# Attention scores in bf16 six-part stacks, and in fp32r three-part stacks with two heads in the row halves of the array

## The reference

```
A:   q, k, v = x @ Wq, x @ Wk, x @ Wv        # 32 query heads, 8 key/value heads, head size 16
     q, k = rope(q), rope(k)
B:   q, k, v = x @ Wq.T + bq, ...            # 32 heads of size 16, no rope
both: scores = q k^T / 4, causal mask, softmax, times v, heads joined, @ Wo
ffn: down(silu(gate(x)) * up(x))             # 4-bit integer weights, a scale per row, low-rank terms
```

## Time and profile before

| | |
|---|---|
| median of three runs | 1965.94 us |
| the profiled execution | 1964.34 us, its span 1962.6 us |
| granted TensorE clock, mean | 0.948 of full |
| TensorE busy (share of span) | 1709.4 us (87%) |
| VectorE | 1132.9 us (58%) |
| ScalarE | 927.3 us (47%) |
| GpSimd | 734.2 us (37%) |
| attention A, f.f., attention B, f.f. | about 0 to 560, 560 to 900, 930 to 1590, 1600 to 1960 us |

### The profile page before, as it was taken

The page is one execution under the profiler, slowest core; times in us unless marked ns, Lnnn a source line. Parts: engine busy times, 40 slices in busy tenths (PEclk is TensorE's granted clock), DMA queues, the critical chain, the costliest instruction groups (busy, mean ns, idle before and its releaser), DMA issues. The chain is left out here.

```text
span 1962.6 us, 34407 instructions
## 1 busy us (share of the span) xinstructions
PE 1709.4 (87%) x11728; PEld 1235.3 (63%) x11728; DVE 1132.9 (58%) x2474; ACT 927.3 (47%) x1740; POOL 734.2 (37%) x2278
## 2 busy tenths in 40 slices
PE   4888989889867999998489899899899967999997
PEld 4555655566535787785366666666667635777785
DVE  5777676676727654543465655665655627655543
ACT  3455555565524454531345545554554625454531
POOL 4455445454411221211445544554554511221211
PEclk8899999999987999999689999999999987999999
DMA  2000100000016211010300000001001016211010
GB/s 98 2 23 13 34 24 18 29 2 30 17 54 192 94 54 65 0 43 22 125 2 2 23 25 22 23 13 34 13 3 43 2 60 188 92 54 64 0 43 22
DMA packets 50485, 81.96 MB, mean 42 GB/s; under 512 B 10123, under 2 KB 22027, under 8 KB 50325
## 3 DMA queue, kind: packets, MB, share of 16 engines
q1 hardware_dynamic: 50324, 79.92, 13.0%
HBM read 62.34 MB, written 16.78 MB: 40 GB/s over the span
## 5 line engine op out<-in xcount | busy, mean ns | idle before, releaser
L247 PE MATMUL f_ring<-f_xt,f_codes 128*128 128x512 f32 (+1 forms) x1408 | 360.2, 398 | 6.4 <-DVEq L1411 5.3
L247 PEld LDWEIGHTS f_ring<-f_xt,f_codes 128*128 128x128 f32 (+1 forms) x1408 | 263.4, 188 | 76.0 <-DVEq L1411 6.1
L1269 POOL TENSOR_TENSOR f_ht<-f_work,f_ht 128x512 fp32r<-128x512 f32 (+1 forms) x88 | 114.5, 1305 | 473.2 <-ACT f_ht L1329 473.2
L767 ACT ACTIVATE ab_region<-ab_scores 128x512 f32<-128x512 f32 x320 | 184.8, 608 | 81.5 <-PE ab_scores L1013 80.2
L767 ACT ACTIVATE aa_region<-aa_scores 128x512 f32<-128x512 f32 x320 | 184.3, 599 | 81.0 <-PE aa_scores L1013 78.2
L1422 DVE TENSOR_TENSOR f_work<-f_ring,f_work 128x512 f32<-128x512 f32 (+1 forms) x176 | 120.5, 689 | 146.0 <-ACT f_work L1318 116.5
L1318 ACT ACTIVATE f_work<-f_ring,f_scales 128x512 f32<-128x512 f32 (+1 forms) x176 | 120.5, 685 | 171.6 <-PE f_ring L247 171.1
L642 POOL TENSOR_SCALAR_AFFINE_SELECT ab_region<-ab_region 128x128 f32<-128x128 f32 x512 | 136.7, 293 | 151.9 <-ACT ab_region L767 151.8
L247 PE MATMUL f_ring<-f_dcodes,f_ht 128*128 128x512 f32 (+1 forms) x704 | 177.2, 407 | 10.2 <-DVE f_down_x L1392 9.3
L642 POOL TENSOR_SCALAR_AFFINE_SELECT aa_region<-aa_region 128x128 f32<-128x128 f32 x512 | 136.5, 295 | 92.5 <-ACT aa_region L767 92.0
L247 PEld LDWEIGHTS f_ring<-f_dcodes,f_ht 128*128 128x128 f32 (+1 forms) x704 | 133.8, 193 | 48.8 <-DVE f_down_x L1392 12.8
(11 more groups left out here) (185 smaller groups left out, 3237.2 us busy)
## 6 DMA issues: line engine op xcount, KB each, us to landing
f_x<-mid SPq DMA_DIRECT2D x32, 256.0 KB, 4.2
f_raw<-mid SPq DMA_DIRECT2D x32, 256.0 KB, 4.3
f_raw<-in_gate_q SPq DMA_DIRECT2D x10, 512.0 KB, 5.5
f_raw<-in_up_q SPq DMA_DIRECT2D x10, 512.0 KB, 4.3
f_raw<-in_down_q SPq DMA_DIRECT2D x10, 512.0 KB, 3.8
aa_x<-in_x SPq DMA_DIRECT2D x16, 256.0 KB, 2.7
aa_res<-in_x SPq DMA_DIRECT2D x16, 256.0 KB, 2.8
mid<-aa_res SPq DMA_DIRECT2D x16, 256.0 KB, 2.0
```

The lines of the kernel that those rows point to most:

```text
L247: mm = pe.matmul(out, w, x, start=start and i == 0, stop=stop and i == len(pairs) - 1)
L767: act.activation(probs[:, s // 2 % 2, SUB * (s % 2) + i, :], scores[:, sbk, :], ACT.Exp, scale=0.25).then_inc(scores_freed[sbk].sem, 1)
L1269: pool.tensor_tensor(ht[0:r, LO, n, :], hid[0:r, n % 2, :], ht[0:r, HI, n, :].bitcast(F32), ALU.subtract).then_inc(hid_lo.sem, 1)
```

## The change

In both attentions q and k are split in two parts of fp32r instead of three of bf16, and three products of parts are laid under one another: 3 x 16 = 48 rows, plus two rows for the maximum in two parts. Two heads of a pair lie in one stack, head 0 in partitions 0 to 49 and head 1 in 64 to 113, so that their products use the upper and the lower half of the array's rows and write different banks. In A, where four query heads share a key head, the key head is written into both halves.

- The staged operand of a pair is [128 tokens, 112] in fp32; a token block has 12 transposes in A (20 before) and 8 in B (16 before), four to a bank, and `stack_out` copies 512 columns.
- ScalarE makes the high parts (two instructions), VectorE the low parts (two), GpSimd the two repeats. The middle part and its steps are gone.
- Scores are made in three groups: both heads' 512 columns at position 0, both heads' 384 and 128 at position 2, both heads' 256 at position 4. A group fills both banks and waits until everything before it has been read. Five exponentials as before; the last reads both banks.
- Maxima are at positions 1 (k = 0, 1), 3 (k = 2, 3) and 4 (k = 4, 5). The masks of both heads come first, with start, and the products of the pair are added. At position 4 the masks come before the scores and the products after them. VectorE reduces k = 0 at position 1, 1 at 2, 2 at 3, and 3, 4, 5 at 4.
- The split of the maxima is two operations; their transpose is an fp32 product with the identity; two DMAs of two rows each place them.

```diff
-PARTS = 6
+PARTS = 3
 STK = PARTS * HD
-MAXROW = STK
-ROWS = STK + 3
+HALF = 64
+ROWS = STK + 2
+SPAN = HALF + STK
+MAXROW = 96
...
-        stacks = sb("stacks", [ROWS, 2, NST, T], BF16)
+        stacks = sb("stacks", [P, 2, NST, T], F32R)
-        staged = sb("staged", [P, NT, NST, PARTS, HD], BF16)
+        staged = sb("staged", [P, NT, NST, SPAN // HD, HD], F32R)
...
+        GROUP = (0, 0, 1, 1, 2)
+        scores_filled = Signal(sem("scores_filled"), 3 * PAIRS)
+        scores_freed = Signal(sem("scores_freed"), SUB * PAIRS, 1)
...
+        MAXIMA_AT = ((2, ()), (2, (0,)), (2, (1,)), (2, (2,)), (2, (3, 4, 5)))
...
-                sp.dma_start(stacks[MAXROW:MAXROW + 3, unit(s) % 2, h:h + 2, :],
-                             rowparts[MAXROW:MAXROW + 24, :]).then_inc(rows_made.sem, 16)
+                for i in range(2):
+                    at = i * HALF + STK
+                    sp.dma_start(stacks[at:at + 2, unit(s) % 2, heads(s, i)[0], :].bitcast(F32),
+                                 rowparts[MAXROW + 8 * i:MAXROW + 8 * i + 8, :].bitcast(F32)).then_inc(rows_made.sem, 16)
...
-                pool.tensor_copy(np_[:, 0], nm).then_inc(nmax_chain.sem, 1)
...
+                pool.tensor_copy(np_[:, :, 0, :], nm).then_inc(nmax_hi.sem, 1)
+                pool.wait_ge(nmax_hi.sem, nmax_hi.at(b, s + 1))
+                pool.tensor_tensor(np_[:, :, 1, :], nm, np_[:, :, 0, :].bitcast(F32), ALU.subtract)\
...
+            def high_parts(t, src):
+                act.copy(in_slot(t, slice(0, HQ), SLOT_HI), q_cols(src))
+                act.copy(in_slot(t, slice(HQ, NST), SLOT_HI), k_cols(src)).then_inc(qk_hi.sem, 1)
...
+            def half(ap, i, rows):
+                return ap[i * HALF:i * HALF + rows]
+
+            def max_blocks(k):
+                return [(qt, P if qt == 1 else 0) for qt in ((0, 1) if k < 2 else (1 + k // 2,))]
+
+            def max_masks(b, s, k0):
+                for k in (k0, k0 + 1):
+                    mb, nth = k % MAXIMA, MB * s + k // MAXIMA
+                    pe.wait_ge(maxima_freed[mb].sem, maxima_freed[mb].at(b, nth))
+                    for n, (qt, at) in enumerate(max_blocks(k)):
+                        pe.matmul(maxima[:, mb, at + qt * P:at + (qt + 1) * P], identb[:], mask_qk[:], start=n == 0,
+                                  stop=False, skip_group_check=True)
+
+            def max_scores(b, s, k0):
+                st = stacks[:, unit(s) % 2]
+                for qt, at in max_blocks(k0):
+                    for k in (k0, k0 + 1):
+                        mb, i, (h, hk, _) = k % MAXIMA, k % 2, heads(s, k % 2)
+                        mm = pe.matmul(maxima[:, mb, at:at + (qt + 1) * P],
+                                       half(st[:, h, qt * P:(qt + 1) * P], i, STK), half(st[:, hk, 0:(qt + 1) * P], i, STK),
+                                       start=False, stop=True, skip_group_check=True)
...
+            def exp_scores(b, s, g):
+                pe.wait_ge(scores_freed.sem, scores_freed.at(b, SUB * s + 2 * g))
...
+                for kb, at in (((0, 0),), ((1, 0), (3, 384)), ((2, 0),))[g]:
+                    for i in range(2):
+                        h, hk, _ = heads(s, i)
+                        mm = pe.matmul(scores[:, i, at:at + T - kb * P], half(st[:, hk, kb * P:(kb + 1) * P], i, ROWS),
+                                       half(st[:, h, kb * P:T], i, ROWS), start=True, stop=True)
+                mm.then_inc(scores_filled.sem, 1)
...
+                        after, k0 = following(region, b, s, 2), {1: 0, 3: 2, 4: 4}.get(i)
+                        if after is not None and k0 is not None:
+                            max_masks(*after, k0)
+                        if i % 2 == 0:
+                            exp_scores(b, s, i // 2)
+                        if after is not None and k0 is not None:
...
+                            max_scores(*after, k0)
```

More of the change, by code:

```diff
@@ L974, in project @@
                 return passes(pe, out, pairs)
[L976 to L991 removed]
+            def half(ap, i, rows):
[17 more added lines that the diff above has]
+                                       start=False, stop=True, skip_group_check=True)
+                        if qt == max_blocks(k)[-1][0]:
+                            mm.then_inc(maxima_filled[mb].sem, 1)
             def max_transposes(b, s):
@@ L1056, in part @@
                         b = b0 + bs
-                        exp_scores(b, s, i)
+                        after, k0 = following(region, b, s, 2), {1: 0, 3: 2, 4: 4}.get(i)
[4 more added lines that the diff above has]
+                        if after is not None and k0 is not None:
+                            if after[1] % STEPS == 0:
+                                banks.all_emptied(pe, where, [("T", unit(after[1]), t, p)
+                                                              for t in ((0, 1), (2,), (3,))[k0 // 2]
+                                                              for p in range(TPARTS)])
+                            max_scores(*after, k0)
                         if i == TRANSPOSE_AT and (after := following(region, b, s, 1)) is not None:
                             max_transposes(*after)
-                        ahead, ks = MAXIMA_AT[i]
-                        if (after := following(region, b, s, ahead)) is not None:
-                            for k in ks:
-                                if k % 2 == 0 and after[1] % STEPS == 0:
-                                    banks.all_emptied(pe, where, [("T", unit(after[1]), t, p)
-                                                                  for t in ((0, 1), (2,), (3,))[k // 2]
-                                                                  for p in range(TPARTS)])
-                                max_scores(*after, k)
                         if i == VALUES_AT and s % 2 == 0 and (before := preceding(region, b, s, 1)) is not None:
@@ L1100, in part @@
                             pe.wait_ge(low_made.sem, low_made.at(b0 + bb, k + 1))
-                        out = banks.take(pe, where, ("T", u, t, p)).bitcast(BF16)
-                        for h in range(min(8, NST - 8 * p)):
-                            src = staged[:, t, 8 * p + h].rearrange("p s d -> p (s d)")
-                            mm = pe.transpose(out[0:STK, h * P:(h + 1) * P], src, identb[:])
+                        out = banks.take(pe, where, ("T", u, t, p))
+                        for h in range(min(4, NST - 4 * p)):
+                            src = staged[:, t, 4 * p + h].rearrange("p s d -> p (s d)").bitcast(F32)
+                            mm = pe.transpose(out[0:SPAN, h * P:(h + 1) * P], src, identf[:])
                         mm.then_inc(banks.is_filled(where, ("T", u, t, p)), 1)
@@ L1109, in part @@
                                                           for t in range(NT) for p in range(TPARTS)])
-                            for k in range(6):
+                            for k in (0, 2, 4):
+                                max_masks(0, 0, k)
                                 max_scores(0, 0, k)
                             max_transposes(0, 0)
-                            for k in range(FIRST):
+                            for k in (0, 2, 4):
+                                max_masks(0, 1, k)
                                 max_scores(0, 1, k)
```

182 lines of the change are left out of this document (67 added, 115 removed).

## The result

The changed kernel takes 2218.28 us (median of 4 runs, 2215.4 to 2223.95) against 1966.28 for the kernel before on the same chip: ratio 1.1285, interval 1.126 to 1.131. I forecast slower, 2037 us; it is slower by 252 us instead of 73, outside the range of 1930 to 2105.

A forecast was written before the change was run, and what follows sets the result against it. TensorE's pace in the two attentions, at a granted clock of 0.95, was taken as the bound. The terms -54 + 21 + 90 + 6 + 20 - 10 = +73 us on 1964.3 gave 2037 us, range 1930 to 2105.

The forecast's parts named there:

- Term 1: Score and maxima products in row halves, both attentions: pairs partly overlap, -54 us; bounds 110 us gain, 44 us loss.
- The rival without overlap: Score and maxima products: the two halves don't run side by side, so +44 instead of -54; 2135 us, chance 0.10.
- Term 2: Transpose of the maxima as a plain fp32 product of 128 columns: 0.23 us instead of 0.06, +21 us.
- Term 3: TensorE switching between whole array and row halves: 940 more changes of tile shape at 0.095 us, +90 us.
- the faster rival: Row halves cost no change of shape and run fully side by side: 1921 us; chance 0.27 with its milder form.
- Term 4: Operand transposes in 32 bits: 1.32 instead of 1.12 us a token block in A, B unchanged; +6 us.
- Term 5: Attention: score groups wait for the previous group's exponentials, masks for the last maxima's reduction; +20 us, bounds 0 and 82.
- the ring: Score banks refilled only after both exponentials of the group before: 4.6 us a step, 15 us over 24 short steps.
- The upper bound of 0.64 us a step: Scores waiting for a whole exponential with its handover in every step, 82 us in all.
- Term 6: Relief of GpSimd in the split of the maxima and staging: its wait of 11.6 us in A halves, likewise B; -10 us.
- The ring rival: Score groups waiting for exponentials become the bound: 2099 us, chance 0.13; sign, 80 us idle on TensorE before scores.
- My last test: Profile after: mechanism wrong if attention gets shorter, or the longer time sits in waits and not in paces.

The follow-up runs named there:

- the last kernel: Kernel before with score products over 128 rows, in A maxima products too, and stacks cleared after the normalisation, 32 bits at a time: 1959.28 us, ratio 0.9965.

## Why the prediction was wrong, step by step

- **Term 1, products in halves: right in size, in part by luck.** Less one change of shape of 0.09 each, the pairs of 512 columns take 0.43 - 0.09 = 0.34 us, of 384 and 128 together 0.35, of 128 and 256 together 0.34, and of 256, with no change behind, 0.22: 1.25 us for six of the eight pairs, where the prediction has 0.24 + 0.44 + 0.44 + 0.22 = 1.34. The 512 alone is dearer than thought, the small ones cheaper. The floor of 0.22 for every pair, taken from 32-bit transposes, is not what shows: it is rather one surcharge of 0.10 to 0.17 us for each group of pairs on top of the columns' own pace (0.34 - 0.24, 0.35 - 0.24, 0.22 - 0.11, 0.34 - 0.17). The rival without overlap is out.
- **Term 2, transpose of the maxima: right.** 476.91 to 477.24 is 0.33 with one change, 0.23 without.
- **Term 3, changes of shape: right.** Four masks and then the maxima take 0.31 us (475.14 to 475.45), three masks at 0.055 leave 0.15. A change to halves costs the same 0.09 as one to columns; the faster rival, which needed it under 0.02, is out.
- **Term 4, operand transposes: a little low.** Four of them, from 488.75 to 489.23, take 0.48 us where I had 0.44; over 224 groups that would be some 9 us more, an estimate from this one group. Terms 1 to 4 made +63 us and the accounting above leaves 65, but that one is good to some 10 us only, so the agreement to 2 us is luck.
- **Term 5, waits: wrong in size, and this is the first step that failed.** "Likewise the masks of the last maxima now wait for the reduction of a bank filled only one position earlier" had the mechanism, but I took it together with the ring at 20 us. I priced the ring with care, and it cost 32 us of waits (20 were taken); the bank wait got no row and no bound of its own, and took 108, where all such waits of the kernel before make 21.5. The row to read was VectorE's: it is 384 of 560 us busy in A, so a reduction waits in its queue behind tasks and one position is not enough. The upper bound of 0.64 us a step was for the wrong wait (and neither it nor the 0.08 of handover was read from a row). Alone, the moved maxima are worth 107 us on the kernel before.
- **Term 6, relief: right or better.** The wait on GpSimd's split is 2.1 us in each attention; I took 10 us off and got some 20.
- **A term that was missing: the granted clock.** I read 0.95 in the earlier trace rows and used the paces of the full clock for the whole sum. The change put 287 us more at half clock, worth about 122 us. One part comes with the idle time (the moved maxima alone: 184 us at half clock); the larger comes with products of 48 and 50 rows, shown by the full-height and 66-row runs. No row of the kernel before could have shown the second: all its large products have 96 rows or more.
- The ring rival's sign that it would show, 80 us before scores, did not come. My last test, "wrong in mechanism if the longer time sits in waits and not in paces", is met in part: 69 us are idle, and the paces are longer mostly because the clock is.

The Trainium skill had a warning that I did not weigh: "TensorEngine Tiling (Array Packing)", Restrictions and Gotchas, says that row tiling raises the pressure on PSUM, since row tiles write different banks. That is the part of the loss that sits in waits: two heads at once need two banks at once, and three were there. "TensorE: Matmul & The Clock Gate" says in its closing table that a product of 32 rows takes as long as one of 128. At one clock the rows here agree (0.22 to 0.23 us for 512 columns, over 48 rows as over 96 and 99), but the clock was not the same.

## What to carry to other kernels

Before pairing work that fills buffers, count the buffers in pairs, and price the reader by its queue (its busy share and what stands ahead of the read), not by the length of one read. Where TensorE's time is the bound, carry a term for the granted clock: products that use few rows of the array can lose as much or more in clock than their overlap wins (2218 us in halves against 2179 at full height here). Rows of zeros that fill up the array cost TensorE no time and can give a little back (7 us of 1966 here at best), if their clearing is kept off the path.

## What the runs showed of the hardware

- The granted clock went with how many rows of the array the products use, with TensorE's instructions and columns the same: half-clock time 292 us with 66 rows, 110 with 96 to 128, and in A 57, 45 and 33 us for scores over 99, over 128, and maxima over 128 too (a step of 0.01 in the granted clock is 11 us here, so these three are coarse; the lengths of A, 566, 560 and 557 us, go the same way). The mean clock of whole runs agrees: 0.907 to 0.916 with 66 rows (4 runs) against 0.947 to 0.951 before (7); 0.950 to 0.954 and 0.952 to 0.955 with 128 rows (6 each) against 0.947 to 0.952 (11); and 0.951 to 0.956 in the last kernel (9) against 0.944 to 0.950 (14).
- Two fp32r products in different row halves overlap almost wholly (0.564 us covered by a pair of 0.560 us each; at full height 0.744 by a pair of 0.455). The first pair after a change of shape takes 0.34 us for 512 columns, 0.1 more than a single product (0.24).
- A change between full height, row halves and narrow column tiles costs 0.09 to 0.10 us each way.
- Clearing 32 partitions x 16384 bf16 on GpSimd takes 13.75 us, and 3 partitions x 4096 take 3.51 in the kernel before: 0.84 and 0.86 ns an element of one partition, so about the same for 32 partitions as for 3. Ahead of the first normalisation it puts TensorE's first product 11 us later.
